# Softmax attention in a four-layer Trainium2 kernel: value products in halves, the rows of maxima turned by TensorE, scores 22 tiles behind the maxima

## The reference, cut to what matters

```
q, k = rope(x_n @ Wq.T + bq), rope(x_n @ Wk.T + bk)      # x_n: x with its rows normed
v = x_n @ Wv.T + bv
for each b and each of 16 heads:
    s = q @ k.T / sqrt(8)                                  # 1024 x 1024
    o = softmax(s) @ v                                     # 1024 x 8
x = x + concat(o) @ Wo.T + bo
```

## Time and profile before

| | |
|---|---|
| Median of 3 runs | 886.65 us (886.46 to 887.2) |
| The profiled execution's own time | 887.39 us |
| Its span in the profile | 886.1 us |
| Mean granted TensorE clock | 0.892 |
| The maxima: first to last reduction starts | 423.35 to 747.83 us |
| Busy: PE, DVE, ACT, POOL | 83%, 75%, 58%, 27% |

### The profile page before, as it was taken

One profiled execution on the slowest core, in us unless ns is written; L12 is line 12 of the kernel. 1 busy time (PEld: TensorE's weight loads), 2 busy tenths in 40 slices (PEclk: granted clock), 3 DMA queues, 4 the chain that ended last, 5 costly groups with the idle time before them and its releaser, 6 DMA issues. The chain is left out here.

```text
span 886.1 us, 18667 instructions
## 1 busy us (share of the span) xinstructions
PE 735.5 (83%) x7088; PEld 359.6 (41%) x7088; DVE 668.5 (75%) x1333; ACT 513.5 (58%) x1012; POOL 237.5 (27%) x295
## 2 busy tenths in 40 slices
PE   6999968888529999909887999999999999956880
PEld 2333246644319999905111222222222222235870
DVE  7878975456875555557886999999999998955555
ACT  3744422564524444454346888888888888943453
POOL 0130010314027766351751200000000000006763
PEclk9999989985758999968658999999999999976995
DMA  3430000000173112133876040404130000023113
GB/s 98 108 85 3 1 23 5 4 3 0 56 281 124 51 47 50 29 104 87 233 155 192 2 86 2 85 3 86 24 64 1 3 2 2 11 88 114 52 48 98
DMA packets 40912, 55.56 MB, mean 63 GB/s; under 512 B 12328, under 2 KB 27824, under 8 KB 40440
## 3 DMA queue, kind: packets, MB, share of 16 engines
q1 hardware_dynamic: 36856, 46.24, 19.6%
q0 software_dynamic: 3968, 8.13, 3.4%
HBM read 35.41 MB, written 14.75 MB: 57 GB/s over the span
## 5 line engine op out<-in xcount | busy, mean ns | idle before, releaser
L1034 DVE TENSOR_REDUCE arena<-psum 128x1 f32<-128x1024 f32 x256 | 300.9, 1217 | 23.7 <-PE psum L918 20.9
L1173 ACT ACTIVATE arena<-psum 128x512 f32<-128x512 f32 x512 | 265.9, 605 | 53.8 <-PE psum L937 53.7
L918 PE MATMUL psum<-arena 56*128 56x512 bf16 x512 | 180.7, 413 | 10.6 <-DVE arena L1034 8.9
L937 PE MATMUL psum<-arena 59*128 59x512 bf16 x512 | 156.2, 389 | 5.5 <-ACT arena L1173 3.6
L948 PE MATMUL psum<-arena 128*32 128x512 f32 x1024 | 138.1, 611 | 8.7 <-issue 8.7
L369 PE MATMUL psum<-arena 128*128 128x128 f32 x808 | 109.5, 284 | 0.4 <-DVE arena L420 0.4
L937 PEld LDWEIGHTS psum<-arena 59*128 59x128 bf16 x512 | 38.4, 94 | 166.0 <-ACT arena L1173 141.2
L369 PEld LDWEIGHTS psum<-arena 128*128 128x128 f32 x808 | 103.4, 200 | 0.7 <-DVE arena L420 0.7
L485 POOL DMA_INDIRECT rows_y<-arena x62 | 61.7, 994 | 38.8 <-DVE arena L434 33.0
L1242 POOL TENSOR_SCALAR arena<-arena 128x16 f32<-128x16 f32 x16 | 4.1, 254 | 249.4 <-DVE arena L1034 249.2
L396 PE MATMUL psum<-arena 128*128 (+1 forms) x496 | 67.5, 280 | 2.4 <-ACT arena L464 1.9
(11 more groups left out here) (312 smaller groups left out, 1056.2 us busy)
## 6 DMA issues: line engine op xcount, KB each, us to landing
arena<-scr_k SPq DMA_DIRECT2D x15, 448.0 KB
arena<-scr_q SPq DMA_DIRECT2D x15, 448.0 KB
arena<-in_f_up SPq DMA_DIRECT2D x1, 4096.0 KB, 14.5
arena<-rows_y SPq DMA_DIRECT2D x12, 256.0 KB, 4.7
scr_q<-arena SPq DMA_DIRECT2D x6, 384.0 KB, 3.3
arena<-in_f_down SPq DMA_DIRECT2D x1, 2048.0 KB, 17.2
arena<-in_f_up SPq DMA_DIRECT2D x1, 2048.0 KB, 9.3
rows_x<-xn SPq DMA_DIRECT2D x5, 256.0 KB, 13.1
```

What stands on the lines that cost most here:

```text
L918: mm = pe.matmul(ps[:, bank + half, :], q[rows, k, h, (qh * 4 + qt) * P:(qh * 4 + qt + 1) * P], kk[rows, k, h, half * BLK:(half + 1) * BLK ...
L937: pe.matmul(ps[:, score_bank(n), :], kk[0:KA, k, h, kb * P:(kb + 1) * P], q[0:KA, k, h, qh * BLK:(qh + 1) * BLK], start=True, stop=True).t ...
L1034: dve.tensor_reduce(mx[:, qh, h * 4 + qt:h * 4 + qt + 1], ps[:, bank:bank + 2, :].rearrange("p a b -> p (a b)"), X, ALU.max).then_inc(S("a ...
L1173: act.activation(pt[:, (u % 3) * HG + h, :], ps[:, score_bank(n), :], ACT.Exp, scale=float(HD) ** -0.5).then_inc(S("a1_exp"), 1)
```

## The change

- AHEAD is 22 instead of 26: scores start four tiles earlier, and 11 units instead of 13 run after the last maxima.
- Within a pair the half of the tile is issued before the score. The value products of unit u - 2 are issued in two halves of 256 query columns, one behind each tile of the unit; the exps and the bank are waited for at the first half. Units without maxima beside them keep the whole product.
- The maxima are turned by a matmul with a bf16 identity (turn_rows) into a bank of the scores' rotation, copied by ACT (rows) into a1_mt [48, 128], and moved by one transfer from SBUF to SBUF. The transpose on DVE, the four stores and the load by way of DRAM are gone. Evictions are counted over scores and turned rows together (TAKEN, bank_of). turn_rows(0) stands after tile 18 of the head, turn_rows(e) in the unit 8e - 2 behind the first half of its value products; ACT's rows(e) behind that unit's second exp.
- q lies as [group, query block, head, 512], so a group's q is loaded in two transfers of 512 columns and k in one: three instead of two.
- leading(6) after unit 0, following(6) after 2, leading(7) after 9, following(7) after 10. POOL has split_rows(1) ahead of rotate(7). On SP max_rows(0) stands ahead of the loads of group 1, max_rows(1) ahead of those of group 2, with the stores of units 4 to 7 between the loads.
- POOL, in the layer before, fills the identity (one copy 128x128) instead of clearing a1_ms.

```diff
-AHEAD = 26
+AHEAD = 22
...
-def score_bank(n):
+def evictions():
+    out = [("rows", 0)]
+    for n in range(G * U * HG):
+        out.append(("score", n))
+        if n % HG == 1 and n // HG % NTB == NTB - 2 and n // HG + 2 < G * U:
+            out.append(("rows", (n // HG + 2) // NTB))
+    return out
+
+TAKEN = {item: i for i, item in enumerate(evictions())}
+FIVE = TAKEN["score", LAST_MAXIMA * HG]
+
+def bank_of(i):
+    return i % 3 if i < FIVE else ((5, 6) + tuple((FIVE + k) % 3 for k in range(3)))[(i - FIVE) % 5]
...
+    def turn_rows(e):
+        i = TAKEN["rows", e]
+        pe.wait_ge(S("a1_split"), e + 1)
...
+        free_bank(i)
+        pe.matmul(ps[0:3 * HG * 4, bank_of(i), 0:P], m["a1_ms"][:].rearrange("p i a -> p (i a)"), m["a1_id"][:],
+                  start=True, stop=True).then_inc(S("a1_s2"), 1)
...
-    def values(u):
+    def values(u, half=None):
...
+        at = slice(0, BLK) if half is None else slice(half * (BLK // 2), (half + 1) * (BLK // 2))
+        if half != 1:
+            if kb == 0:
+                pe.wait_ge(S("a1_va"), st + 1)
+                if u >= NTB:
+                    pe.wait_ge(S("a1_o"), u // NTB)
+            pe.wait_ge(S("a1_exp"), TAKEN["score", u * HG + HG - 1] + 1)
         for h in range(HG):
-            mm = pe.matmul(ps[32 * h:32 * h + 32, 7, :], va[:, kb, (st % NG) * HG + h, :],
-                           pt[:, (u % 3) * HG + h, :], start=kb == 0, stop=kb == NTB - 1, skip_group_check=True)
-        mm.then_inc(S("a1_pv"), 1)
+            mm = pe.matmul(ps[32 * h:32 * h + 32, 7, at], va[:, kb, (st % NG) * HG + h, :],
+                           pt[:, (u % 3) * HG + h, at], start=kb == 0 and half != 1, stop=kb == NTB - 1, skip_group_check=True)
+        if half != 0:
+            mm.then_inc(S("a1_pv"), 1)
...
     for n in range(AHEAD):
         max_half(n, 0)
         max_half(n, 1)
+        if n == 2 * NTB + 2:
+            turn_rows(0)
     for u in range(G * U):
         beside = tiles_before(u)
         for i, n in enumerate(beside or (None, None)):
-            scores(u, 2 * i)
-            if n is not None:
-                max_half(n, 0)
-            scores(u, 2 * i + 1)
-            if n is not None:
-                max_half(n, 1)
-            if i == 0 and u >= 2:
-                values(u - 2)
+            for half in range(2):
+                if n is not None:
+                    max_half(n, half)
+                scores(u, 2 * i + half)
+            if u >= 2 and (beside or i == 0):
+                values(u - 2, i if beside else None)
+            if i == 0 and u % NTB == NTB - 2 and u + 2 < G * U:
+                turn_rows((u + 2) // NTB)
...
-    def max_rows(e):
-        dve.wait_ge(S("a1_split"), e + 1)
-        if e:
-            dve.wait_ge(S("a1_ms"), 64 * e)
-        dve.transpose(mt[:].rearrange("p a b -> p (a b)"), msp[:].rearrange("p a b -> p (a b)")).then_inc(S("a1_mc"), 1)
...
+    def rows(e):
+        i = TAKEN["rows", e]
+        act.wait_ge(S("a1_s2"), i + 1)
+        if e:
+            act.wait_ge(S(f"a1_mrow{(e - 1) % 2}"), 16 * ((e - 1) // 2 + 1))
+        act.copy(m["a1_mt"][0:3 * HG * 4, :], ps[0:3 * HG * 4, bank_of(i), 0:P]).then_inc(S("a1_exp"), 1)
...
     def max_rows(e):
         g, qh = e // 2, e % 2
-        sp.wait_ge(S("a1_mc"), e + 1)
-        for r in range(4):
-            sp.dma_start(scr_m[qh, :, :, r, :].rearrange("a i j -> i a j"), mt[32 * r:32 * r + 16]).then_inc(S("a1_ms"), 16)
-        sp.wait_ge(S("a1_ms"), 64 * (e + 1))
-        sp.dma_start(q[KR:KA, g % NG, :, qh * BLK:(qh + 1) * BLK],
-                     scr_m[qh].rearrange("a (h t) r j -> a h (t r j)", h=HG)).then_inc(S(f"a1_mrow{qh}"), 16)
+        sp.wait_ge(S("a1_exp"), TAKEN["rows", e] + 1)
+        sp.dma_start(q[KR:KA, g % NG, qh].rearrange("i h t -> i (h t)"), mt[0:3 * HG * 4, :]).then_inc(S(f"a1_mrow{qh}"), 16)
...
+    group(0, 0, "a1_two0")
+    group(S1B, 1, "a1_one1")
+    max_rows(0)
+    group(0, 1, "a1_two1")
+    group(S1B, 2, "a1_one2")
+    store_all(4)
     max_rows(1)
+    group(0, 2, "a1_two2")
+    store_all(5)
+    group(S1B, 3, "a1_one3")
+    max_rows(2)
+    group(0, 3, "a1_two3")
+    store_all(6)
     store_all(7)
-    max_rows(2)
```

More of the change, by code:

```diff
@@ L23 @@
 TABLES_AT = 45672
-AHEAD_AT = TABLES_AT - 12336 - 3076
+AHEAD_AT = TABLES_AT - 12376 - 3076
 WORDS = 46192
@@ L810, with before_in_bank @@
 LAST_MAXIMA = (TILES - AHEAD + 1) // 2 + 1
[L813 to L821 removed]
+def evictions():
[9 more added lines that the diff above has]
+    return i % 3 if i < FIVE else ((5, 6) + tuple((FIVE + k) % 3 for k in range(3)))[(i - FIVE) % 5]
+def before_in_bank(i):
+    return max((k for k in range(max(0, i - 5), i) if bank_of(k) == bank_of(i)), default=None)
 def attn1_memory(c, w):
@@ L917, in max_half @@
         rows = slice(S1B, S1B + KR)
-        mm = pe.matmul(ps[:, bank + half, :], q[rows, k, h, (qh * 4 + qt) * P:(qh * 4 + qt + 1) * P],
+        mm = pe.matmul(ps[:, bank + half, :], q[rows, k, qh, h, qt * P:(qt + 1) * P],
                        kk[rows, k, h, half * BLK:(half + 1) * BLK], start=True, stop=True)
@@ L1052, in attn1_dve @@
         max_tile(n)
-        if n >= 19 and (n - 19) % 16 == 0:
-            max_rows((n - 19) // 16)
-    max_rows(2 * G - 1)
     o, rd, halves, rows = m["a1_o"], m["a1_rd"], G * QH, m["xn"][:].rearrange("p t d -> p (t d)")
@@ L1165, in attn1_act @@
         following(n)
-    leading(6)
+    def rows(e):
[4 more added lines that the diff above has]
+        act.copy(m["a1_mt"][0:3 * HG * 4, :], ps[0:3 * HG * 4, bank_of(i), 0:P]).then_inc(S("a1_exp"), 1)
+    rows(0)
     for u in range(G * U):
         for h in range(HG):
-            n = u * HG + h
-            act.wait_ge(S("a1_s2"), n + 1)
+            i = TAKEN["score", u * HG + h]
+            act.wait_ge(S("a1_s2"), i + 1)
             if h == 0 and u >= 3:
                 act.wait_ge(S("a1_pv"), u - 2)
-            act.activation(pt[:, (u % 3) * HG + h, :], ps[:, score_bank(n), :], ACT.Exp, scale=float(HD) ** -0.5).then_inc(S("a1_exp"), 1)
+            act.activation(pt[:, (u % 3) * HG + h, :], ps[:, bank_of(i), :], ACT.Exp, scale=float(HD) ** -0.5).then_inc(S("a1_exp"), 1)
+            if h == 1 and u % NTB == NTB - 2 and u + 2 < G * U:
+                rows((u + 2) // NTB)
         if u == 0:
+            leading(6)
+        if u == 2:
             following(6)
-        if u == 4:
+        if u == 9:
             leading(7)
-        if u == 5:
+        if u == 10:
             following(7)
@@ L1225, in rotate @@
         pool.wait_ge(S("a1_r0"), n + 1)
-        subtract(n)
     def values(st):
@@ L1254, in attn1_pool @@
     rotate(4)
+    subtract(4)
     pool.wait_ge(S("a1_v"), NB)
@@ L1258, in attn1_pool @@
     rotate(5)
+    subtract(5)
     split_rows(0)
     rotate(6)
+    subtract(6)
+    split_rows(1)
     rotate(7)
-    split_rows(1)
+    subtract(7)
     split_rows(2)
@@ L1324, in attn1_sp @@
         what, b = UNITS1[n]
-        load(what, S1B, 0, block[b], block[b], "a1_first")
+        if what == 0:
+            load_q(S1B, 0, 0, b, "a1_first")
+        else:
+            load(1, S1B, 0, block[b], kk[S1B:S1B + KR, 0, :, block[b]], "a1_first")
     store(0, 2, others, "a1_st")
@@ L1331, in attn1_sp @@
     sp.wait_ge(S("a1_st3"), 48)
-    load(0, S1B, 0, block[1], block[1], "a1_second")
+    load_q(S1B, 0, 0, 1, "a1_second")
     for n in range(FIRST):
         sp.wait_ge(S(f"a1_st{n}"), 48)
-    for g in range(NG):
-        group(0, g, f"a1_two{g}")
-        if g + 1 < NG:
-            group(S1B, g + 1, f"a1_one{g + 1}")
-        if g == 1:
-            max_rows(0)
-    for n in range(4, 7):
-        store_all(n)
-    max_rows(1)
+    group(0, 0, "a1_two0")
[4 more added lines that the diff above has]
+    store_all(4)
+    max_rows(1)
+    group(0, 2, "a1_two2")
[4 more added lines that the diff above has]
+    store_all(6)
     store_all(7)
-    max_rows(2)
     for e in range(3, 2 * G):
```

69 lines of the change are left out of this document (32 added, 37 removed).

## The result

The changed kernel takes **859.0 us** (median of 4 runs, 858.17 to 860.77); before, on the same chip, 886.92. The ratio is 0.9671 [0.9625, 0.9718]. On another chip it was 858.29 against 885.88, 0.9673 [0.964, 0.9705]. The profiled execution has an own time of 860.77 us, a span of 859.0 and a mean granted clock of 0.903.

A forecast was written before the change was run, and what follows sets the result against it. DVE was taken as the frame, made to wait by PE's order. Savings 17.3 + 9.1 + 2.0 = 28.4 from 887.39 leave 859.0; the median, 0.74 lower, is 858.2 us. Range 852 to 869.

The forecast's parts named there:

- Part 1: Tile 47 to tile 255: thirteen blocks at 18.5 us instead of 19.83 save 17.3 us.
- The wait for bank 7: At each block's end, the first half product waits for ACT's copy of bank 7 and starts 0.4 us late.
- spreads the stall: Middle: DVE's reserve (pair ready 0.6 us after its banks are free, needed after 1.14) spreads PE's stall.
- Part 2: The start, up to tile 47: tile 47 comes at 480.8 instead of 489.9, saving 9.1 us, bounds 7 and 11.
- the climb of the clock: Start: full clock 3.8 us after value products begin; until then some two tiles lose 1.3 us together.
- Part 3: The end, after the last reduction's start: four tiles less of lag save 2.0 us, bounds 1.5 and 3.9.
- keeps its length: End: everything behind PE's first output product (units 122 to 127, output) takes as long as before.
- merely waits longer: End: PE, with two units less in front of its first output product, only waits longer for DVE, about 2 us.
- clock 1.00 from 458 on without a fall: Sign to look for: PE's granted clock stays full from 458 us onward.
- (a): Rival, middle: halves cost more than half, a tile 1.24 us, the stretch saves nothing: 875.5 us, chance 0.10.
- (b): Rival, middle: DVE's pace rules, PE's waits fit its reserve, 18.2 us a block: 853.3 us, chance 0.15.
- (d): Rival: turned rows' transfer exceeds its 2.9 us, PE pays 15 times, a loss from 4.8 us on; chance 0.03.

The follow-up runs named there:

- w1_slow_way: The changed kernel with one more transfer of the same 12 KB to DRAM, waited for, ahead of the turned rows' transfer: 880.52 us, 884.63 before.
- b3_halves_head: The kernel before with only the value products in halves and the moved steps of the start: 856.85 us, 884.63 before.
- t2_filled: The changed kernel with five matmuls of no use filling PE's wait ahead of the first output product: 884.34 us, 913.06 before.
- s1_whole: The changed kernel with whole value products behind a unit's first tile instead of halves: 909.51 us, 913.06 before.
- t1_out_later: The changed kernel with the first two output products on PE two units later: 884.44 us, 913.06 before.

## Why the prediction was right, and where it was not

**Part 1, the middle: 17.3 predicted, 18.5 measured.** Each term stands against a row. A half: 0.56, measured 0.57. A tile on PE: 1.12, measured 1.107. turn_rows: 0.2, measured 0.24. The wait for bank 7: 0.4, measured 1.53 - 1.107 = 0.42, and 0.03 in the tile behind. The sum on PE was to be 18.5 and is 16 x 1.107 + 0.24 + 0.42 + 0.03 = 18.4; "PE, not DVE, is then the tighter by 0.3" held (18.41 to 16 x 1.133 = 18.13). The remaining 1.2 us is 13 blocks times 0.09. (The upper bound given as 19.0 is 18.9 by its own terms, 17.9 + 0.35 + 0.65.) What was said of the reserve was wrong: DVE's reserve "spreads the stall" into a shorter one, but doesn't shorten the block, as w1_slow_way shows. It does absorb the wait where DVE is the tighter, as in b3_halves_head.

**Part 2, the start: 9.1 predicted, 10.0 measured.** Tile 22 was put at 449.7 and came at 449.52, tile 47 at 480.8 and came at 479.78. turn_rows(0) cost 0.47 for 0.6, casts and copy 0.70 for 0.7. Mis-sized was the climb of the clock: 3.8 us behind the first value products, taken from the place behind the long stall, and 2.2 measured (454.11 to 456.3). In the kernel before it was 3.4 behind the very first value products (460.01 to 463.4), and 1.5 to 4.9 over all kernels, so no single row could have given it. The half clock cost one stall of 0.75, not 1.3, and tile 28 starts one pitch behind 456.19, at 457.3 and not 458.1.

**Part 3, the end: 2.0 predicted, 2.6 lost. This step failed.** The prediction had DVE's place right: turn_back's transpose ends at T + 13.69 before and at T + 11.85 after, 1.8 us earlier; the first output product moved by 14.02 - 11.91 = 2.1. But it read the earlier trace rows wrongly. PE did not wait for DVE there: the transpose ended at 761.52, PE came to the product at 761.85, by its own order, and had no idle time. So after the change PE waits at this place for the first time. What failed is the sentence that all behind it "keeps its length", and with it that PE "merely waits longer", and the sign to look for, "clock 1.00 from 458 on without a fall". A wait is not only its own length: this one of 1.11 us (about 2 had been foreseen) is what t2_filled had to fill for the clock to stay, and the half clock that came with it cost 4.7. The prediction had used the same mechanism at the start, and not at the place where it had itself added idle time. T + 29.16 less 2.1 is 27.06, where t2_filled, with the clock held, has 27.02.

That the total came out right is luck: 1.2 and 1.1 too little in parts 1 and 2 (the first reduction's 0.2 included), and 1.0 behind the stage, stand against the 4.6 too much in part 3.

**The rivals.** (a) Halves that cost much more than half: refuted, by 0.57 a half (the rival's tile of 1.24 needs 0.68) and by s1_whole, where whole products make the block 20.05. The Trainium skill, TensorEngine Tiling, Performance Considerations (Instruction Overhead), gives about 60 cycles of overhead for each matmul, by the prediction's estimate 0.2 us a unit for the eight records that halves add; this trace has 2 x 0.57 - 0.99 = 0.15, not far from it. The 20.1 of the prediction came from adding that 0.2 to a sum in which each half already carried its 0.12. (b) DVE's pace rules: true of b3_halves_head (18.37), not of the changed kernel. (c), (d) Turned rows late: only the last of the 16 transfers, expected 0.5 us ahead of need, held PE. A weight load stood 0.61 us for it, and the unit took 0.28 more. The 2.9 us from issue to need were right (3.00 measured), as was the price of 1 us by the block for each above (w1_slow_way); with 2.23 from issue to PE's start the slack is only 0.77, and a store by way of DRAM ahead of the transfer already uses it up.

**Left open.** What makes one wait bring the fall and another not: 1.11 and 1.24 us ahead of the output products did, 1.05 ahead of value products near the same place (t1_out_later) and 1.26 in the middle (w1_slow_way) did not. Whether the output products behind the wait have a part in it was not tried. The 1.0 us behind the stage is not explained. The price read from w1_slow_way rests on one profile.

## What to carry to other kernels

Add up each engine's work in one period from the distances of its starts: the second engine's sum shows what freeing the first can bring, here nothing, since 18.37 on DVE was replaced by 18.41 on PE. Cut a long product in front of a time-critical pair into pieces as long as the gap: that alone brings 19.9 us of the stage, where the whole change brings 25.9. And where an edit makes PE wait, even for one microsecond, read the granted clock behind it; if it falls, fill the wait with other work or with dummy matmuls, or move the work that waits. Whether PE waits is read from PE's own rows, not from the queue of weight loads.
